# Masks and biases written into PSUM banks by ScalarE, and TensorE's turn rotated, in an attention and feed-forward kernel

## The chip, the cores and the metric

The kernel runs on one core of a Trainium2 chip. The metric is the device time of one execution in microseconds. Engines are named as in the profile: PE (TensorE), DVE (VectorE), ACT (ScalarE), POOL (GpSimd), SP (the queue that issues DMAs). "Bank" is one of PE's eight result banks in PSUM, 128 partitions by 512 words of fp32.

## The reference, cut to what matters

Tokens come from an image tensor (512 x 8 rows) and a text tensor (77 x 8 rows): 4712 tokens with 256 features. Three steps follow, each with fp32 weights.

```python
h = einsum('bhid,oi,od->bho', x, weighted_sum, weight)       # image tokens
h = concatenate([h, txt], axis=1)
# attention over the 8 batch entries of one token position, 16 heads of 16
qkv = layernorm(h) @ in_w.T + in_b;  q, k, v = split(qkv)
att = softmax(einsum(norm(q), norm(k)) * exp(min(logit_scale, log 100)))
h = h + ((att @ v) * head_scale) @ out_w.T + out_b
# feed-forward: attention among the 16 heads of one token, then 8 gated experts
y = layernorm(h);  g = rmsnorm(y) * gamma1
q = g @ Wq + bq;  k, v = split((g @ Wdown + bdown) @ Wup + bup)
x2 = y + (softmax(q k^T / 4) v) @ Wo + bo
h2 = rmsnorm(x2) * gamma2;  gate = softmax(h2 @ Wg + bg)
out = h + x2 + sum_e gate_e * (h2 @ We_e)
```

In both steps a token attends to a few others only: in the first to the 8 rows of its own position, in the second a head to the heads of its own token. The kernel computes scores for blocks of 32 rows and adds a mask of -2^120 to the scores that don't belong.

## The kernel before, in words

The 4712 tokens are cut into 37 tiles of 128 rows. The program has three parts: the first makes the image tokens and splits the weights into a high and a low fp16 part; the second runs the attention step over all tiles; the third runs the feed-forward step. A product in fp32 accuracy is three fp16 products (`product`, lines 173 to 179), two chunks of 128 features each, so six matmuls.

The second and third part are software pipelines with the order written by hand. Each engine has its own function `body(i, p)`, run once a turn by `tiles_in_order` (line 59): a few turns unrolled ahead, a hardware loop over the middle, the rest unrolled behind. In turn `i` an engine works on several tiles at different depths; `real(i, k)` is true where tile `i + k` exists. Every engine carries out its own list strictly in order, and waits on counters (semaphores) with `wait_ge`; there is no planner. In the last turns of the attention part each engine appends the first turns of the feed-forward part (`in_tail`, turns 35 and later).

Attention, turn `i`, on PE (lines 885 to 923): for tile i a mask product into bank b_s (L889, 4 rows by 512 columns in bf16, with `start=True`), on top of it the scores (L881, 64 small 32x32-tile matmuls); the output product of tile i-2 (rows_times, L176 to L178); transposes of xn of tile i+3 (L904); the weighted sums of tile i-1 (L871, 128 small ones); the product that makes q and k of tile i+2 into b_qk, ended by the bias product (L185, ones by the bias row, 3 rows by 512 columns); the V product of tile i+2 into b_v; the transposes of on of tile i-1 (L920). ACT (lines 935 to 964) makes xn, the exp (L946), the square and the copy of q and k out of b_qk (L950, L952), the high half of xn transposed (xt_h, L956), the high half of on transposed (on_t_h, L960) and the V copy (vaug, L964). DVE (lines 978 to 1056) makes the maximum (smax, L981), the subtraction (sc, L992), the transposes, the normalisation and the low halves (on_t_l L1053, xt_l L1056); POOL does three Newton steps for the norms (L1076).

Feed-forward, turn `i`, on PE (lines 604 to 669): the mask product of tile i into bank b_s3 (L607) and the first half of the scores (L589); the transposes of on of tile i-1 (L616); the q product of tile i+1; the second half of the scores; then the four expert products of tile i-2 with the other small products between them, the transposes of h (L655) and of hn (L661), and last the gate product of tile i-1 (with its bias, L185). ACT: on_t_h (L678), qraw (L682), the exp (L686), lat (L690) and lat_h (L694) of tile i+1, and more. DVE: on_t_l (L750), smax (L754), sc (L757), the expert sums (acc and res, L742), lat_l (L763), pr_t, x, fq_t, kv_t, v, h (L789), of (L793), h_t_l (L798), on (L803), hn_l, hn, the gate's maximum and normalisation.

Of the kernel before, what the change touches and what calls it, by code (L numbers as in the profile page):

```python
# [86 lines left out]
def build(nc, x, txt, wst_in, w_rep, in_w, logit, head, out_w, g1, wq, wd, bd, wu, bu, bv, bo, bq,  # L87
          wo, g2, wg, we, biases, bscale_c, ident_c, amask_c, fmask_c, out):
    with ExitStack() as ctx, ExitStack() as phase1:
# [44 lines left out]
        v48 = [sb(f"v48_{p}", [P, 16, 48]) for p in range(2)]  # L134

# [37 lines left out]
        def product(dst, a_h, a_l, b_h, b_l, chunks, start=True, stop=True):  # L173

            for c in range(chunks):
                nc.tensor.matmul(dst, a_h(c), b_h(c), start=start and c == 0, stop=False)  # L176
                nc.tensor.matmul(dst, a_h(c), b_l(c), start=False, stop=False)  # L177
                last = nc.tensor.matmul(dst, a_l(c), b_h(c), start=False, stop=stop and c == chunks - 1)  # L178
            return last

        def rows_times(dst, t_h, t_l, w_h, w_l, bias=None):

            last = product(dst, lambda c: t_h[:, c, :], lambda c: t_l[:, c, :], w_h, w_l, KC, stop=bias is None)
            if bias is not None:
                last = nc.tensor.matmul(dst, ones3[:, :], brow[:, bias], start=False, stop=True)  # L185
            return last
# [49 lines left out]
        with nc.Block() as block:  # L236
# [215 lines left out]
            def _(pe):  # L452
# [13 lines left out]
                for i in range(IMG_TILES):  # L466
# [57 lines left out]
                 "bvec_ps", "bvec_ready")  # L524
# [3 lines left out]
         bvec_ps, bvec_ready) = map(sem, names)  # L528
# [5 lines left out]
        def ffn_coefficients(pool, j):  # L534
# [31 lines left out]
                 "f_gmul", "f_we", "f_comb", "f_acc", "f_x1", "p_x1", "p_hx2", "p_t2", "p_r2", "out_done")  # L566
# [3 lines left out]
         f_gmul, f_we, f_comb, f_acc, f_x1, p_x1, p_hx2, p_t2, p_r2, out_done) = map(sem, names)  # L570
# [5 lines left out]
        def ffn_pe(pe):  # L576
# [27 lines left out]
            def body(i, p):  # L604
                if real(i, 0):
                    pe.wait_ge(f_qt, i + 1)
                    nc.tensor.matmul(b_s3[:, :], fm[:, 0:P], fm[:, P:], start=True, stop=True,  # L607
                                     skip_group_check=True)
                    scores(range(0, 8))
                if real(i, -1):  # L610
                    pe.wait_ge(f_on, i)
                    wait(pe, f_h2l, i - 1)
                    if real(i, 0):
                        pe.wait_ge(f_lat, i + 1)
                    for c in range(KC):
# [57 lines left out]
        def ffn_act(act):  # L673
            def body(i, p):
# [182 lines left out]
        with nc.Block() as block:  # L857
            @block.tensor
            def _(pe):
# [25 lines left out]
                def body(i, p):  # L885
                    if real(i, 0):
                        pe.wait_ge(a_qkt, i + 1)
                        wait(pe, a_sub, i)
                        nc.tensor.matmul(b_s[:, :], am[:, 0:P], am[:, P:], start=True, stop=True,  # L889
                                         skip_group_check=True)  # L890
                        scores(range(0, 4))
# [16 lines left out]
                    if real(i, 2):  # L908
                        pe.wait_ge(a_xtl, i + 3)
                        wait(pe, a_qkr, i + 2)  # L910
                        rows_times(b_qk[:, :], xt_h, xt_l, lambda c: inw_h[:, c, 0:2 * D],
                                   lambda c: inw_l[:, c, 0:2 * D], slice(0, 2 * D)).then_inc(a_qkm, 1)
                    if real(i, 2):
                        wait(pe, a_v, i + 2)
                        rows_times(b_v[:, 0:D], xt_h, xt_l, lambda c: inw_h[:, c, 2 * D:3 * D],
                                   lambda c: inw_l[:, c, 2 * D:3 * D]).then_inc(a_vm, 1)
                    if real(i, -1):
                        pe.wait_ge(a_on, i)
                        for c in range(KC):
# [7 lines left out]
                           slice(3 * D, 4 * D)).then_inc(bvec_ps, 1)  # L927
                head = ffn_pe(pe)
# [3 lines left out]
            def _(act):  # L932
                nc.scalar.activation(ls[:, :], ls[:, :], ACT.Exp).then_inc(ls_ready, 1)

                def body(i, p):
                    if real(i, 3):
# [5 lines left out]
                                             scale=cf_all[:, at, RS:RS + 1].squeeze(1)).then_inc(a_xn, 1)  # L942
                    if real(i, 0):
                        act.wait_ge(a_sub, i + 1)
                        wait(act, a_prt, i)
                        nc.scalar.activation(pr[:, :, :], sc[:, :, :], ACT.Exp).then_inc(a_exp, 1)  # L946
                    if real(i, 2):
# [4 lines left out]
                        nc.scalar.activation(qkr[(p + 2) % 3][:, :], b_qk[:, :], ACT.Copy, scale=1.0 / WS).then_inc(a_qkr, 1)  # L952
                    if real(i, 3):
# [235 lines left out]
```

## Time and profile before

| | us |
|---|---|
| median of 3 runs | 916.53 |
| lowest, highest | 912.55, 917.62 |
| the profiled execution | 916.73 |
| its span | 914.9 |

Over that span PE is busy 808.9 us (88%), DVE 787.8 (86%), POOL 398.9 (44%), ACT 321.7 (35%). The first part lasts until about 100 us, attention until about 390, feed-forward from about 410 to the end, with a mixed stretch between them. A matmul's end is modelled, so two neighbours on PE may overlap in the rows. "PEclk" is TensorE's granted clock, 1.00 for 2.4 GHz.

### The profile page before, as it was taken

Reading aid. Unit: us, or ns where it says so; the run is one execution under the profiler, and the core shown is the slowest. Engines: PE = TensorE matmul, PEld = TensorE weight load, DVE = VectorE, ACT = ScalarE, POOL = GpSimd, SP = SyncE. Lnnn points to the kernel's source line nnn. Section 1 sums busy time; section 2 is a strip of 40 time slices with the busy share of each in tenths; the row PEclk is TensorE's granted clock in tenths of the full one; section 3 lists DMA queues with packets and bytes.
Section 4 is the critical chain, followed back from the end, with each engine's and each line's share of the span. In section 5 each row is a group of like instructions: output and inputs, shape, how many; then the busy total and the mean of one; then the engine's idle time right before and its main releaser. Section 6 shows DMA issues by size and latency. Waiting matters only on the chain.

```text
span 914.9 us, 48709 instructions
## 1 busy us (share of the span) xinstructions
PE 808.9 (88%) x20422; PEld 517.0 (57%) x20422; DVE 787.8 (86%) x1847; ACT 321.7 (35%) x797; POOL 398.9 (44%) x1122
## 2 busy tenths in 40 slices
PE   4999788888888888776999999999999999999997
PEld 3888455555555555444555555555555555555553
DVE  5898479999999999856789999999999999999996
ACT  4576334444444444212222322332233223322321
POOL 1421255555555555644334444434443344434111
PEclk9999989999999999857899999999999999999999
DMA  9973000000000000000000000000000000000000
GB/s 324 312 239 110 2 3 4 0 0 0 0 0 0 0 0 1 4 2 4 9 10 13 12 11 6 11 11 11 6 11 11 11 6 11 11 6 11 12 16 17
DMA packets 16692, 28.14 MB, mean 31 GB/s; under 512 B 3425, under 2 KB 11953, under 8 KB 16632
## 3 DMA queue, kind: packets, MB, share of 16 engines
q1 hardware_dynamic: 16632, 27.28, 9.0%
q8 instruction: 45, 0.74, 0.3%
q14 instruction: 15, 0.12, 0.0%
HBM read 22.44 MB, written 4.83 MB: 30 GB/s over the span
## 4 chain that ended last, share of the span: by engine, by line
DVE 27%; PE 15%; issue 10%; ACT 3%; DVEq 1%; POOL 1%; ACTq 0%; POOLq 0%
PE bank L589 6%; DVE acc L742 5%; DVE fq_t L778 3%; DVE h L789 3%; DVE smax L754 3%; DVE sc L757 3%; DVE pr_t L767 2%; DVE of L793 2%; PE bank L176 2%; DVE kv_t L780 2%; PE bank L177 2%; PE bank L178 1%; DVE x L774 1%; PE bank L616 1%; DVE h_t_l L798 1%
## 5 line engine op out<-in xcount | busy, mean ns | idle before, releaser
L833 POOL TENSOR_TENSOR qpad<-qraw,bq_s 128x256 f32<-128x256 f32 x37 | 26.8, 725 | 200.7 <-ACT qraw L682 200.7
L176 PE MATMUL bank<-we_h,h_t_h 128*128 128x512 f16 x296 | 113.8, 384 | 0.0
L177 PE MATMUL bank<-we_l,h_t_h 128*128 128x512 f16 x296 | 112.7, 381 | 0.0
L178 PE MATMUL bank<-we_h,h_t_l 128*128 128x512 f16 x296 | 112.5, 380 | 0.0
L742 DVE SCALAR_TENSOR_TENSOR acc<-bank,gate,acc 128x256 f32<-128x256 f32 x222 | 105.1, 474 | 5.1 <-PE bank L178 1.1
L176 PE MATMUL bank<-tokw_h,x_t_h 128*128 128x256 f16 x256 | 70.7, 276 | 12.2 <-DVE x_t_l L371 12.2
L177 PE MATMUL bank<-tokw_l,x_t_h 128*128 128x256 f16 x256 | 70.6, 276 | 0.0
L178 PE MATMUL bank<-tokw_h,x_t_l 128*128 128x256 f16 x256 | 70.5, 276 | 0.0
L600 PEld LDWEIGHTS bank<-pr_t,v 32*32 32x32 f32 x4736 | 48.0, 106 | 33.0 <-issue 33.0
L1076 POOL TENSOR_TENSOR rt<-rn 128x32 f32<-128x32 f32 x111 | 26.7, 240 | 84.7 <-DVE rn L1048 78.9
L946 ACT ACTIVATE pr<-sc 128x512 f32<-128x512 f32 x37 | 23.3, 630 | 108.0 <-DVE sc L992 108.0
L589 PEld LDWEIGHTS bank<-kv_t,fq_t 32*32 32x32 f32 x4736 | 49.3, 108 | 18.4 <-issue 18.4
L589 PE MATMUL bank<-kv_t,fq_t 32*32 32x32 f32 x4736 | 57.9, 196 | 0.6 <-issue 0.6
L600 PE MATMUL bank<-pr_t,v 32*32 32x32 f32 x4736 | 56.2, 195 | 2.4 <-issue 2.4
L871 PE MATMUL bank<-vaug,pr_t 32*32 32x17 f32 x4736 | 49.3, 183 | 4.2 <-issue 4.2
L871 PEld LDWEIGHTS bank<-vaug,pr_t 32*32 32x32 f32 x4736 | 45.2, 108 | 9.8 <-issue 9.8
L176 PE MATMUL bank<-inw_h,xt_h 128*128 128x512 f16 (+1 forms) x148 | 50.5, 341 | 0.0
L178 PE MATMUL bank<-inw_h,xt_l 128*128 128x512 f16 (+1 forms) x148 | 49.9, 337 | 0.0
L177 PE MATMUL bank<-inw_l,xt_h 128*128 128x512 f16 (+1 forms) x148 | 49.8, 336 | 0.0
L178 PEld LDWEIGHTS bank<-we_h,h_t_l 128*128 128x128 f16 x296 | 29.1, 98 | 35.3 <-issue 0.6
L712 ACT ACTIVATE h_t_h<-bank 128x256 f16<-128x256 f32 x37 | 14.2, 384 | 95.9 <-PE bank L655 95.9
L371 DVE TENSOR_TENSOR x_t_l<-xbuf,x_t_h 128x1024 f16<-128x1024 f32 x32 | 39.5, 1239 | 8.4 <-ACT x_t_h L294 8.4
(204 smaller groups left out, 2275.5 us busy)
## 6 DMA issues: line engine op xcount, KB each, us to landing
xbuf<-in_x SPq DMA_DIRECT2D x32, 512.0 KB, 4.6
out<-res SPq DMA_DIRECT2D x36, 128.0 KB
we_s<-in_we SPq DMA_DIRECT2D x4, 512.0 KB, 5.6
inw<-in_in_w SPq DMA_DIRECT2D x1, 768.0 KB, 11.4
wrep<-in_w_rep SPq DMA_DIRECT2D x1, 512.0 KB, 5.4
h_all<-in_txt SPq DMA_DIRECT2D x1, 512.0 KB
wst<-in_wst_in SPq DMA_DIRECT2D x1, 256.0 KB, 2.8
outw<-in_out_w SPq DMA_DIRECT2D x1, 256.0 KB, 10.6
```

Of the source, the lines that this page charges most:

```text
L176: nc.tensor.matmul(dst, a_h(c), b_h(c), start=start and c == 0, stop=False)
L177: nc.tensor.matmul(dst, a_h(c), b_l(c), start=False, stop=False)
L178: last = nc.tensor.matmul(dst, a_l(c), b_h(c), start=False, stop=stop and c == chunks - 1)
L371: nc.vector.tensor_tensor(x_t[i % XT][1][:, :, :], xbuf[i % XB][:, :, :], x_t[i % XT][0][:, :, :], ALU.subtract).then_inc(lo_ready, 1)
L589: last = nc.tensor.matmul(b_s3[q, pair * 32:pair * 32 + 32], fq_t[q, 2 * pair:2 * pair + 2, :].rearrange("r t h -> r (t h)"), kv_t[q, :, 2 ...
L600: last = nc.tensor.matmul(b_o3[q, pair * 32:pair * 32 + 32], v48[p][q, pair, 16:48], pr_t[0][q, pair, :], start=True, stop=True)
L742: op = nc.vector.scalar_tensor_tensor(out=(res if e == E - 1 else acc)[:, :], in0=b_we[s % 2][:, k * D:(k + 1) * D], scalar=gate[p][:, e:e ...
L754: nc.vector.tensor_reduce(smax[:, :], s3, AX.X, ALU.max).then_inc(f_max, 1)
L757: nc.vector.tensor_tensor(sc[:, :, :], s3, smax[:, :].unsqueeze(2).to_broadcast([P, 16, 32]), ALU.subtract).then_inc(f_sub, 1)
L778: nc.vector.transpose(fq_t[:, :, :].rearrange("r t h -> r h t"), qpad[:, :, :])
L789: nc.vector.tensor_scalar(h2[:, :], x2[:, :], r2[:, :], None, ALU.mult).then_inc(f_h2, 1)
L871: last = nc.tensor.matmul(b_o[q, h * 17:h * 17 + 17], pr_t[(p + 2) % 3][q, h, :], vaug[(p + 2) % 3][q, h, :], start=True, stop=True)
```

## The change

Three tiles are added in SBUF: `amask`, `fmask`, `qkbias` (128 x 512 fp32). Ahead of the attention loops PE makes each mask and the bias of q and k once, as a product into a bank, and ACT copies them out to SBUF. In the loops ACT copies them from SBUF into the bank before PE's next product into it, and PE's products add onto that (`onto=True`: no `start`). In attention the mask copy follows the exp, and the bias copy follows the copy of q and k; the mask copy of the feed-forward part follows its exp and is ahead of lat. The mask product of the feed-forward part stays for tile 0. PE's order is rotated: in attention the V product (and ACT's copy of it) moves from the end of a turn to the start of the next, behind the transposes of on; in the feed-forward part the transposes of on come ahead of the first half of the scores. DVE, POOL and SP keep their lists.

```diff
+        amask = sb("amask", [P, 512])
+        fmask = sb("fmask", [P, 512])
+        qkbias = sb("qkbias", [P, 512])
...
-        def rows_times(dst, t_h, t_l, w_h, w_l, bias=None):
+        def rows_times(dst, t_h, t_l, w_h, w_l, bias=None, onto=False):
-            last = product(dst, lambda c: t_h[:, c, :], lambda c: t_l[:, c, :], w_h, w_l, KC, stop=bias is None)
+            last = product(dst, lambda c: t_h[:, c, :], lambda c: t_l[:, c, :], w_h, w_l, KC, start=not onto,
+                           stop=bias is None, onto=onto)
...
@@ ffn_pe body
-                if real(i, 0):
-                    pe.wait_ge(f_qt, i + 1)
-                    nc.tensor.matmul(b_s3[:, :], fm[:, 0:P], fm[:, P:], start=True, stop=True,
-                                     skip_group_check=True)
-                    scores(range(0, 8))
                 if real(i, -1):
                     pe.wait_ge(f_on, i)
...
                     last.then_inc(f_onps, 1)
+                if real(i, 0):
+                    settle(pe, c_in)
+                    pe.wait_ge(f_qt, i + 1)
+                    if isinstance(i, int) and i == 0:
+                        nc.tensor.matmul(b_s3[:, :], fm[:, 0:P], fm[:, P:], start=True, stop=True,
+                                         skip_group_check=True)
+                    else:
+                        pe.wait_ge(f_mask, i)
+                    scores(range(0, 8))
@@ ffn_act body, between the exp (L686) and lat (L690)
+                if real(i, 0) and real(i, 1):
+                    act.wait_ge(f_sub, i + 1)
+                    nc.scalar.activation(b_s3[:, :], fmask[:, :], ACT.Copy).then_inc(f_mask, 1)
@@ attention, PE body
+                    if real(i, 1):
+                        wait(pe, a_v, i + 1)
+                        rows_times(b_v[:, 0:D], xt_h, xt_l, lambda c: inw_h[:, c, 2 * D:3 * D],
+                                   lambda c: inw_l[:, c, 2 * D:3 * D]).then_inc(a_vm, 1)
                     if real(i, 0):
+                        settle(pe, c_in)
                         pe.wait_ge(a_qkt, i + 1)
-                        wait(pe, a_sub, i)
-                        nc.tensor.matmul(b_s[:, :], am[:, 0:P], am[:, P:], start=True, stop=True,
-                                         skip_group_check=True)
+                        pe.wait_ge(a_mask, i + 1)
                         scores(range(0, 4))
...
-                        wait(pe, a_qkr, i + 2)
+                        pe.wait_ge(a_bias, i + 3)
                         rows_times(b_qk[:, :], xt_h, xt_l, lambda c: inw_h[:, c, 0:2 * D],
-                                   lambda c: inw_l[:, c, 0:2 * D], slice(0, 2 * D)).then_inc(a_qkm, 1)
-                    if real(i, 2):
-                        wait(pe, a_v, i + 2)
-                        rows_times(b_v[:, 0:D], ...).then_inc(a_vm, 1)
+                                   lambda c: inw_l[:, c, 0:2 * D], onto=True).then_inc(a_qkm, 1)
@@ attention, PE and ACT ahead of the loops
+                nc.tensor.matmul(b_s[:, :], am[:, 0:P], am[:, P:], start=True, stop=True)
+                nc.tensor.matmul(b_ot[:, :], fm[:, 0:P], fm[:, P:], start=True, stop=True)
+                nc.tensor.matmul(b_qk[:, :], ones3[:, :], brow[:, 0:2 * D], start=True, stop=True).then_inc(mask_ps, 1)
...
+                act.wait_ge(mask_ps, 1)
+                nc.scalar.activation(qkbias[:, :], b_qk[:, :], ACT.Copy)
+                nc.scalar.activation(amask[:, :], b_s[:, :], ACT.Copy)
+                nc.scalar.activation(fmask[:, :], b_ot[:, :], ACT.Copy).then_inc(mask_ready, 1)
+                act.wait_ge(mask_ready, 1)
@@ attention, ACT body
+                    if real(i, 1):
+                        act.wait_ge(a_vm, i + 2)
+                        wait(act, a_av, i - 1)
+                        nc.scalar.activation(vaug[(p + 1) % 3][:, :, 0:HD], b_v[:, 0:D], ACT.Copy, scale=1.0 / WS).then_inc(a_v, 1)
                     if real(i, 0):
...
                         nc.scalar.activation(pr[:, :, :], sc[:, :, :], ACT.Exp).then_inc(a_exp, 1)
+                    if real(i, 1):
+                        wait(act, a_sub, i + 1)
+                        nc.scalar.activation(b_s[:, :], amask[:, :], ACT.Copy).then_inc(a_mask, 1)
...
+                    if real(i, 3):
+                        wait(act, a_qkr, i + 3)
+                        nc.scalar.activation(b_qk[:, :], qkbias[:, :], ACT.Copy).then_inc(a_bias, 1)
...
-                    if real(i, 2):
-                        act.wait_ge(a_vm, i + 3)
-                        wait(act, a_av, i)
-                        nc.scalar.activation(vaug[(p + 2) % 3][:, :, 0:HD], b_v[:, 0:D], ACT.Copy, scale=1.0 / WS).then_inc(a_v, 1)
```

## Rows read from the trace of the kernel before

**Rows 1.** The page: busy us (share of the span) xinstructions; the granted clock in 40 slices.

```profile
PE 808.9 (88%) x20422; PEld 517.0 (57%) x20422; DVE 787.8 (86%) x1847; ACT 321.7 (35%) x797; POOL 398.9 (44%) x1122
...
PEclk9999989999999999857899999999999999999999
```

**Rows 2.** The chain of waits, two feed-forward turns: start us, us, what.

```profile
506.98 0.70 DVE smax L754
...
508.97 0.35 ACT lat L690
...
509.35 0.32 ACT lat_h L694
...
509.69 0.04 DVE lat_l L763
...
516.53 0.37 DVE h_t_l L798
...
517.44 0.38 PE bank L607
...
533.39 0.70 DVE smax L754
```

**Rows 3.** Waits of DVE in 470 to 880: waited for, us in total, times, longest us.

```profile
DVE smax L754 <- PE bank L589: 11.2, 31, 0.5
DVE lat_l L763 <- ACT lat_h L694: 5.2, 17, 0.3
DVE on_t_l L750 <- ACT on_t_h L678: 3.6, 15, 0.3
```

**Rows 4.** The timeline of a feed-forward turn: start us, us, engine line op.

```profile
508.43 0.63 ACT L686 ACTIVATE pr<-sc 128x512 f32<-128x512 f32 x1 [1.76 <-DVE sc L757]
...
517.75 0.75 PE L589 MATMUL bank<-kv_t,fq_t 32*32 32x32 f32 x64
...
519.53 0.42 DVE L750 TENSOR_TENSOR on_t_l<-bank,on_t_h 128x256 f16<-128x256 f32 x1 [0.24 <-ACT on_t_h L678]
...
520.27 0.69 DVE L754 TENSOR_REDUCE smax<-bank 128x16 f32<-128x512 f32 x1 [0.31 <-PE bank L589]
```

**Rows 5.** The timeline of an attention turn.

```profile
250.42 1.10 PE L881 MATMUL bank<-k_t,q_t 32*32 32x64 f32 x64
...
251.91 0.69 DVE L981 TENSOR_REDUCE smax<-bank 128x16 f32<-128x512 f32 x1
...
255.62 0.28 PE L176 MATMUL bank<-inw_h,xt_h 128*128 128x256 f16 x1
...
256.17 0.27 PE L178 MATMUL bank<-inw_h,xt_l 128*128 128x256 f16 x1
256.27 0.41 DVE L1028 TENSOR_TENSOR on<-bank,rsum 128x256 f32<-128x256 f32 x1
...
256.73 0.44 PE L920 MATMUL bank<-ident,on 128*128 128x128 f32 x2 [0.29 <-DVE on L1028]
...
258.75 0.42 DVE L1053 TENSOR_TENSOR on_t_l<-bank,on_t_h 128x256 f16<-128x256 f32 x1
...
259.42 0.68 DVE L981 TENSOR_REDUCE smax<-bank 128x16 f32<-128x512 f32 x1
```

**Rows 6.** Groups by line and shape: busy us, mean ns, idle before.

```profile
L952 ACT ACTIVATE qkr<-bank 128x512 f32<-128x512 f32 x37 | 21.9, 592 | 0.0
```

**Rows 7.** The timeline ahead of the loops.

```profile
100.09 0.59 ACT L940 ACTIVATE xn<-h_all,cf_all 128x256 f32<-128x256 f32 x1
...
100.95 0.44 PE L904 MATMUL bank<-ident,xn 128*128 128x128 f32 x2
```

**Rows 8.** Busy us (xinstructions) of each engine, then clock and DMA, in three stretches.

```profile
372.60:376.60 4.00, 2.37 (x136) 1.87 (x137) 3.58 (x11) 0.63 (x1) 2.91 (x13) 1.00 0.01 4
376.60:379.60 3.00, 3.00 (x9) 0.92 (x8) 2.09 (x5) 0.28 (x1) 1.40 (x2) 0.53 0.02 5
256.20:260.20 4.00, 3.07 (x78) 1.98 (x75) 3.80 (x11) 2.11 (x6) 1.73 (x5) 1.00 0.00 0
```

More of the change, by code:

```diff
@@ L171, in build, with product @@
         bank = [ctx.enter_context(nc.psum_tensor(f"bank{n}", [P, 512], F32)) for n in range(8)]
-        def product(dst, a_h, a_l, b_h, b_l, chunks, start=True, stop=True):
+        def product(dst, a_h, a_l, b_h, b_l, chunks, start=True, stop=True, onto=False):
             for c in range(chunks):
-                nc.tensor.matmul(dst, a_h(c), b_h(c), start=start and c == 0, stop=False)
-                nc.tensor.matmul(dst, a_h(c), b_l(c), start=False, stop=False)
-                last = nc.tensor.matmul(dst, a_l(c), b_h(c), start=False, stop=stop and c == chunks - 1)
-            return last
-        def rows_times(dst, t_h, t_l, w_h, w_l, bias=None):
-            last = product(dst, lambda c: t_h[:, c, :], lambda c: t_l[:, c, :], w_h, w_l, KC, stop=bias is None)
+                nc.tensor.matmul(dst, a_h(c), b_h(c), start=start and c == 0, stop=False, skip_group_check=onto)
+                nc.tensor.matmul(dst, a_h(c), b_l(c), start=False, stop=False, skip_group_check=onto)
+                last = nc.tensor.matmul(dst, a_l(c), b_h(c), start=False, stop=stop and c == chunks - 1,
+                                        skip_group_check=onto)
+            return last
+        def rows_times(dst, t_h, t_l, w_h, w_l, bias=None, onto=False):
+            last = product(dst, lambda c: t_h[:, c, :], lambda c: t_l[:, c, :], w_h, w_l, KC, start=not onto,
+                           stop=bias is None, onto=onto)
             if bias is not None:
@@ L523, in build @@
                  "a_on", "a_onps", "a_onh", "a_onl", "a_out", "a_h", "a_st", "a_mv", "a_keep", "p_newton", "p_rn", "p_kpad", "p_bias",
-                 "bvec_ps", "bvec_ready")
+                 "bvec_ps", "bvec_ready", "mask_ps", "mask_ready", "a_mask", "a_bias")
         (ls_ready, a_xn, a_xnps, a_xth, a_xtl, a_qkm, a_vm, a_sq, a_qkr, a_v, a_ss, a_half,
@@ L527, in build @@
          a_on, a_onps, a_onh, a_onl, a_out, a_h, a_st, a_mv, a_keep, p_newton, p_rn, p_kpad, p_bias,
-         bvec_ps, bvec_ready) = map(sem, names)
+         bvec_ps, bvec_ready, mask_ps, mask_ready, a_mask, a_bias) = map(sem, names)
         b_xt, b_qk, b_v, b_s, b_o, b_ot, b_out = bank[0:7]
@@ L565, in build @@
                  "f_wo", "f_x2", "f_ss2", "f_h2", "f_h2ps", "f_h2h", "f_h2l", "f_gate", "f_gmax", "f_gexp", "f_grec",
-                 "f_gmul", "f_we", "f_comb", "f_acc", "f_x1", "p_x1", "p_hx2", "p_t2", "p_r2", "out_done")
+                 "f_gmul", "f_we", "f_comb", "f_acc", "f_x1", "p_x1", "p_hx2", "p_t2", "p_r2", "f_mask", "out_done")
         (f_hn, f_hnps, f_hth, f_htl, f_q, f_down, f_lat, f_lath, f_latl, f_qraw, f_qpad, f_kv, f_kvt, f_qt,
@@ L569, in build @@
          f_wo, f_x2, f_ss2, f_h2, f_h2ps, f_h2h, f_h2l, f_gate, f_gmax, f_gexp, f_grec,
-         f_gmul, f_we, f_comb, f_acc, f_x1, p_x1, p_hx2, p_t2, p_r2, out_done) = map(sem, names)
+         f_gmul, f_we, f_comb, f_acc, f_x1, p_x1, p_hx2, p_t2, p_r2, f_mask, out_done) = map(sem, names)
         b_turn, b_q, b_kv, b_we, b_s3, b_o3, b_hn = bank[0], bank[1], bank[2], bank[3:5], bank[5], bank[6], bank[7]
@@ L909, in body @@
                         pe.wait_ge(a_xtl, i + 3)
-                        wait(pe, a_qkr, i + 2)
+                        pe.wait_ge(a_bias, i + 3)
                         rows_times(b_qk[:, :], xt_h, xt_l, lambda c: inw_h[:, c, 0:2 * D],
-                                   lambda c: inw_l[:, c, 0:2 * D], slice(0, 2 * D)).then_inc(a_qkm, 1)
-                    if real(i, 2):
-                        wait(pe, a_v, i + 2)
-                        rows_times(b_v[:, 0:D], xt_h, xt_l, lambda c: inw_h[:, c, 2 * D:3 * D],
-                                   lambda c: inw_l[:, c, 2 * D:3 * D]).then_inc(a_vm, 1)
+                                   lambda c: inw_l[:, c, 0:2 * D], onto=True).then_inc(a_qkm, 1)
                     if real(i, -1):
```

## The prediction

> **What bounds the kernel now.** I began with the page: how busy each engine is, and the clock that TensorE was granted. PE is busy 88% of the span, DVE 86%, ACT 35% [rows 1]. So PE and DVE both look nearly full, and ScalarE looks free. That is an average over two long stages, and a thing moved to a free engine costs nothing only where nobody waits for that engine. So I read one turn of each stage.
>
> *Second stage (feed-forward), from about 410 us to the end.* The chain of waits repeats every turn. Two turns go from a smax start at 506.98 to one at 533.39, 13.2 us each [rows 2]. In each turn the chain runs smax, sc on DVE, then **ACT's exp, lat and lat_h**, and back to DVE at lat_l. From there it stays on DVE to h_t_l, crosses to PE for the gate product, the mask product (L607), the first half of the scores, the transposes, the q product and the second half of the scores, and ends at the next smax. The reader is to see two things. The mask product is on the chain. And so is ScalarE, exactly once, between exp and lat_h: lat starts 0.54 us after exp starts and lat_l starts as lat_h ends [rows 2, 4]. DVE's waits say the same: in the steady stretch DVE waited 11.2 us in 31 turns for PE's scores, 5.2 us in 17 turns for lat_h, and 3.6 us in 15 turns for on_t_h [rows 3]. In the turns without a shown wait at lat_l, lat_h ends just as DVE gets there.
>
> *First stage (attention), about 112 to 390 us.* One turn takes 7.51 us (smax at 251.91 and at 259.42) [rows 5]. The scores end at 251.52 (250.42 plus 1.10) and smax starts 0.39 later, because DVE is still at earlier work. PE in its turn is idle 0.29 us ahead of the transposes of on, waiting for DVE. DVE sets the pace here, with almost no wait of its own.
>
> **The change part by part.** No DMA is added, removed or moved.
>
> (a) *Feed-forward mask copy, placed between exp and lat on ScalarE.* It runs in 36 turns (tiles 0 to 35; the next tile's mask). Its wait (f_sub) is already met when exp starts, so it follows exp at once. Behind it in ScalarE's queue are lat and lat_h, and for those waits DVE at lat_l; behind lat_l stand pr_t, two acc, x, fq_t, kv_t, v, h, two acc, of, h_t_l, all on the chain. So what the copy takes is added to the turn in full. The trace has no ScalarE write into a bank. The nearest row by shape and source is exp, 512 elements from SBUF: 0.63 us long, with the next operation 0.54 us after its start [rows 2, 4], an overlap of 0.09. The ends: a 512-element copy of 0.592 us out of a bank [rows 6], less the same overlap, is 0.50; exp's full 0.63 if nothing overlaps. A gain is excluded, since ScalarE does one thing at a time. I take 0.54, as exp shares the source: 36 x 0.54 = **+19.4 us** (18.0 to 22.7).
>
> The Trainium skill (ScalarE: Activation LUTs, "Step-by-step: what each stage is for") says that a ScalarE result goes faster into PSUM than into SBUF, and under "What ACT_TABLE_LOAD costs" it gives 186 ns + 0.833 ns per element, less about 93 ns between neighbours: an estimate of 0.52 us from that page, or 18.7 us in 36 turns. No row here shows a write to a bank.
>
> (b) *Feed-forward mask product gone from 36 turns, the transposes of on put ahead of the scores.* L607 starts at 517.44, the scores at 517.75: 0.31 [rows 2, 4]. Nothing else of PE's segment goes; two transposes and eight groups of scores change places. The transposes can start when on is ready, which it is by the end of the gate product, so the swap itself costs about nothing. It helps once: the transposes no longer stand behind 0.7 us of scores, so on_t_h is there before DVE wants it and the 0.24 us wait at on_t_l goes. What is late next is still PE: with the scores 0.31 earlier, smax can start at 519.96 instead of 520.27, while DVE, ready for on_t_l at 519.29, would have been done at 519.71 [rows 4]. So of the two improvements only PE's counts, and I take 0.30 per turn. The ends: 0.21, if going from transposes to the small score tiles costs PE some 0.1 more than from L607 to them; 0.38, all of L607. 36 x 0.30 = 10.8; two of these turns run while the clock is low [rows 1], where L607 costs about twice, 0.5 more: **-11.3 us** (7.6 to 13.7).
>
> (c) *Attention: mask product and bias product gone from PE, two copies added on ScalarE.* PE's work falls by about 0.3 + 0.3 us a turn. Since the scores already end 0.39 ahead of smax [rows 5], DVE gains nothing. The mask copy stands behind exp and ahead of the square of q and k, which waits for PE's product anyway; the bias copy fills a stretch in which ScalarE would wait for V. Cost 0.
>
> (d) *Attention rotation: the V product moves behind the transposes of on.* After the q/k product PE has nothing until DVE's on ends at 256.68 (256.27 plus 0.41); the transposes start at 256.73; V takes 0.82 (255.62 to 256.17 plus 0.27) [rows 5] and would run 257.02 to 257.85. Queued behind V is xt_h on ScalarE, behind xt_h is on_t_h, and for that waits DVE at on_t_l, 258.75 [rows 5]. xt_h would start about 257.9, on_t_h 0.28 later, ending 258.55: 0.2 us before DVE wants it. The cover is thin but there. If it were gone, each 0.1 us missing costs 3.4 us in 34 turns. I take 0, with ends of -1 (less traffic) and +4.
>
> (e) *Before the loops.* ScalarE's first xn starts at 100.09 now [rows 7]. After the change it stands behind three copies, which wait for three more products on PE. PE is free for these at 100.95, where the first transposes start now [rows 7]. Three products of 512 columns with about 0.25 between starts and 0.38 for the last end near 101.85. Three copies at 0.54, 0.54 and 0.6 end near 103.5, and xn follows: **+3.4 us** (3.1 to 3.8). Every engine stands idle for it, nothing hides it.
>
> (f) *Filling and draining the pipeline.* There PE's products are on the path: two bias products, and three or four mask products, at 0.3 each at full clock and up to 0.5 at half. About half of them should count: **-1.5 us** (-2.5 to 0).
>
> Sum: 19.4 - 11.3 + 0 + 3.4 - 1.5 = +10.0 us. The profiled execution took 916.73 (its span is 914.9, and 1.8 lies around it); the median of the runs shown is 916.53, 0.2 less. Forecast: 926.7 on the first footing, **926.5 us** as a median.
>
> **The rivals.**
>
> *1. PE is the bound of the feed-forward stage, and the result is faster.* The mechanism: the 0.5 us that lat_l comes later is absorbed in DVE's queue before h_t_l, so only (b) counts. For it: PE is busy 88% against DVE's 86% [rows 1], and it is the scores that DVE waits for most [rows 3]. Against it: the chain has no wait between lat_l (509.69) and h_t_l (516.53) in which DVE is free [rows 2]. It would decide if DVE had over 0.24 us of slack there. Time: 916.5 - 11.3 + 3.4 - 1.5 = 907.
>
> *2. The two sides of the feed-forward turn cancel.* Copy at 0.50, PE's segment shorter by 0.38, and the fill and drain gain their full 2.5: 18.0 - 13.7 + 3.1 - 2.5 = +4.9, or 921; another microsecond from the attention stage gives 920, inside 0.5%.
>
> *3. The attention stage slows down by its rotation.* on_t_h comes 0.2 us after DVE wants it rather than before. Then each of 34 turns costs 0.2: 926.5 + 7 = 933. For it: two more copies in ScalarE's queue, and a thin cover. Against it: the arithmetic of (d).
>
> *4. TensorE's clock falls in the attention stage.* Ahead of a fall from 2.4 to 1.2 GHz near the end of this stage PE was busy 2.37 of 4.00 us; an idle-rich stretch of a steady turn has 3.07 of 4.00, at a granted clock of 1.00 [rows 8]. The change takes the mask product out of just that stretch and puts an idle 1.3 us (255.4 to 256.7) ahead of the transposes, some 0.3 us less work than now. That goes towards the stretch that fell without reaching it. At half clock PE's turn would take about 10 us instead of 7.5; ten such turns cost 25 us: 951. The Trainium skill (TensorE: Matmul & The Clock Gate, its Part 1, the HAM clock gate) says that the throttled state is the default and that activity releases it; the fall behind the emptier stretch agrees.
>
> That the copies would not do what they say (a bank's sum not starting from what ScalarE wrote) would change the numbers, not the time.
>
> **How the numbers follow.** The forecast gets 0.69, rival 1 0.09, rival 2 0.08, rival 3 0.09, rival 4 0.05. What a measurement of this kernel can tell from no change is about 0.5%, 4.6 us. The forecast's own ends are +3.9 (18.0 - 13.7 + 3.1 - 2.5 - 1) and +22.9 (22.7 - 7.6 + 3.8 + 4), 920.4 to 939.4, which are all bad luck on one side; its middle takes in 921 to 934. The range is 919 to 936: it holds the forecast but for its far end, rival 2 and rival 3, and leaves out rivals 1 and 4. Slower by over 0.5%: nearly all of the forecast, rivals 3 and 4, a little of rival 2: 0.81. Within 0.5%: most of rival 2, the low end of the forecast, a part of rival 1: 0.11. Faster: 0.08.
>
> **What would show each step.** (a): the copy in the feed-forward turn lasting 0.55 to 0.63 us; lat starting 1.0 to 1.1 us after exp instead of 0.54; DVE waiting for lat_h in every turn, 0.5 to 0.8 us each, the largest of its waits. (b): DVE's waits for on_t_h gone, those for the scores still there; PE's segment from h_t_l to smax 0.3 shorter. Both: a feed-forward turn of about 13.45 us. (c), (d): an attention turn of 7.5 to 7.6 us, no new wait of DVE in it, on_t_l without idle before it. (e): the first xn near 103.5. The prediction is wrong if the feed-forward turn is not longer than 13.2 us, if DVE's wait at lat_l has not grown, if the attention turn changes by more than 0.1 us, or if the granted clock leaves 1.0 in a stage where it was steady.

## The result, and the profile after

The changed kernel takes 939.0 us (median of 4, 937.4 to 939.8); the kernel before 915.4 beside it (median of 4). The ratio is 1.0263, 95% interval 1.0236 to 1.0289: slower by about 24 us. Medians and ratios, here and below, leave out the few executions in which the chip was in a slower state. The direction was forecast, the size was not: 926.5 us, range 919 to 936. The profiled execution took 938.91 us with a span of 937.1, 22.2 more than before.

The page, busy times and granted clock:

```profile
PE 781.1 (83%) x20315; PEld 512.9 (55%) x20315; DVE 787.2 (84%) x1847; ACT 380.1 (41%) x910; POOL 396.4 (42%) x1122
...
PEclk9999889999999999755999999999999999999999
```

Against [rows 1], PE lost 28 us of work and ScalarE took on 58, as the change says, and the span grew by 22.

The chain of waits over two feed-forward turns (start us, us, what):

```profile
527.68 0.70 DVE smax L766
...
529.67 0.58 ACT bank L698
530.25 0.29 ACT lat L702
...
530.57 0.32 ACT lat_h L706
...
530.91 0.04 DVE lat_l L775
...
537.83 0.37 DVE h_t_l L810
...
538.65 0.37 PE bank L616 x2
539.02 0.68 PE bank L594 x55
539.71 0.08 issue
539.78 0.27 PE bank L179
...
540.60 0.70 PE bank L594 x56
...
541.33 0.70 DVE smax L766
...
555.08 0.70 DVE smax L766
```

A turn is 13.65 and 13.75 us here against 13.2 in [rows 2]. The new entry is `ACT bank L698`, the mask copy, between exp and lat. From a smax to its lat_l it is 3.23 us (527.68 to 530.91); in [rows 2] it was 2.71 (506.98 to 509.69). That is 0.52 more, in every turn. The other half of the turn is the surprise: from h_t_l's start to the next smax it was 3.74 (516.53 to 520.27, [rows 2, 4]) and 3.50 in the other kind of turn, and is 3.50 (537.83 to 541.33) and 3.73 now. The mask product is gone from that stretch and nothing became shorter.

The waits of DVE in 480 to 900 us (us in total, times, longest), to be held against [rows 3]:

```profile
DVE lat_l L775 <- ACT lat_h L706: 21.1, 30, 0.8
DVE smax L766 <- PE bank L594: 12.2, 31, 1.6
DVE acc L754 <- PE bank L181: 3.5, 14, 0.3
DVE on_t_l L762 <- issue: 3.4, 14, 0.3
```

The wait at lat_l has gone from 5.2 us in 17 turns to 21.1 in 30: it is now the largest. The wait for PE's scores is as large as before. The 0.24 us ahead of on_t_l is still there, and its releaser is now "issue": what DVE waits for there, in one turn of two, is nothing on another engine. Run 12 below ties it to the jump of DVE's own loop.

The timeline of an attention turn, as in [rows 5]:

```profile
301.70 0.69 DVE L1006 TENSOR_REDUCE smax<-bank 128x16 f32<-128x512 f32 x1
...
305.98 0.41 DVE L1053 TENSOR_TENSOR on<-bank,rsum 128x256 f32<-128x256 f32 x1
...
306.45 0.44 PE L931 MATMUL bank<-ident,on 128*128 128x128 f32 x2 [1.29 <-DVE on L1053]
...
307.27 0.27 PE L181 MATMUL bank<-inw_h,xt_l 128*128 128x256 f16 x1
...
307.92 0.38 ACT L989 ACTIVATE on_t_h<-bank 128x256 f16<-128x256 f32 x1
...
308.46 0.42 DVE L1078 TENSOR_TENSOR on_t_l<-bank,on_t_h 128x256 f16<-128x256 f32 x1
...
309.13 0.68 DVE L1006 TENSOR_REDUCE smax<-bank 128x16 f32<-128x512 f32 x1
```

The turn is 7.43 between these two smax, and 7.564 on average over turns 14 to 32, against 7.567 before. PE's idle time ahead of the transposes of on is 1.29 us, V ends at 307.54, on_t_h ends at 308.30 and DVE takes it at 308.46: the thin cover held, with 0.16 us to spare.

Ahead of the loops, and the first stretch of the attention part (timeline; then busy times, granted clock 0.76, DMA):

```profile
101.36 0.60 ACT L949 ACTIVATE qkbias<-bank 128x512 f32<-128x512 f32 x1 [1.53 <-PE bank L941]
...
102.33 0.60 ACT L951 ACTIVATE fmask<-bank 128x512 f32<-128x512 f32 x1
102.97 0.60 ACT L959 ACTIVATE xn<-h_all,cf_all 128x256 f32<-128x256 f32 x1
...
103.62 0.68 PE L919 MATMUL bank<-ident,xn 128*128 128x128 f32 x2 [2.30 <-ACT xn L959]
...
105.78 0.63 PE L179 MATMUL bank<-inw_h,xt_h 128*128 128x512 f16 x1
```

```profile
100.00:120.00 20.00, 12.00 (x108) 6.37 (x106) 7.30 (x18) 9.69 (x21) 7.07 (x23) 0.76 0.00 1
```

The first xn starts at 102.97, 2.88 later than in [rows 7]. But the first smax of the attention part is at 118.38 against 114.12, 4.26 later. The further 1.4 us come with the clock, as far as the rows show; no run separates the two. PE stood idle 2.3 us for the copies, and its first q/k and V products run at half clock: the granted clock is 0.50 from 104 to 110, a matmul takes 0.63 us that took 0.38 before, and from the first of these products to the end of the last it is 4.1 us instead of 2.5. The kernel before has a low stretch as well, but it is shorter and in the second tile's products (granted clock 0.78, 0.50 and 0.87 in the three 2 us windows from 106); the changed kernel has a second one from 116 to 120 (0.83, 0.50).

### The profile page after: what moved, and what is told of

It is laid out like the page before. It is cut to its first block, busy times and chain, and to the rows that moved or that the text cites. A ratio compares the mean times of both kernels' runs of the same rounds, so it can differ in the third digit from the quotient of the medians.

```text
span 937.1 us, 48668 instructions
## 1 busy us (share of the span) xinstructions
PE 781.1 (83%) x20315; PEld 512.9 (55%) x20315; DVE 787.2 (84%) x1847; ACT 380.1 (41%) x910; POOL 396.4 (42%) x1122
## 4 chain that ended last, share of the span: by engine, by line
DVE 27%; PE 13%; issue 10%; ACT 5%; DVEq 1%; POOL 1%; ACTq 0%; POOLq 0%
PE bank L594 6%; DVE acc L754 5%; DVE fq_t L790 3%; DVE h L801 3%; DVE smax L766 3%; DVE sc L769 3%; DVE pr_t L779 3%; PE bank L179 2%; DVE of L805 2%; ACT bank L698 2%; DVE kv_t L792 2%; PE bank L616 2%; DVE x L786 1%; DVE h_t_l L810 1%; PE bank L181 1%
## 5 line engine op out<-in xcount | busy, mean ns | idle before, releaser
L931 PE MATMUL bank<-ident,on 128*128 128x128 f32 x74 | 17.3, 318 | 47.5 <-DVE on L1053 47.5
L969 ACT ACTIVATE pr<-sc 128x512 f32<-128x512 f32 x37 | 23.3, 630 | 77.4 <-DVE sc L1017 77.4
L695 ACT ACTIVATE pr<-sc 128x512 f32<-128x512 f32 x37 | 23.3, 630 | 68.1 <-DVE sc L769 68.1
```

## The experiments

"Turn" is the mean feed-forward turn: the start of smax in turn 33 less that in turn 5, divided by 28. "Inner" and "edge" are the two kinds of turn: PE's hardware loop is two turns long, and an edge turn is one whose first operation comes behind the loop's jump. The columns after them give where, in us from the first gate product of the turn, PE starts the first scores and the q product, and DVE the next smax (from one turn of each kind in the timeline; inner / edge).

Five of the means hold turns that are 0.59 us shorter for a reason of their own, which the last section shows: one such turn in the changed kernel, in run 1 and in run 8, two in run 6, three in run 12. Without them the means are 13.70 (changed), 13.18 (run 1), 13.07 (run 8), 13.20 (run 6) and 13.16 (run 12).

| kernel | turn | scores | q product | smax |
|---|---|---|---|---|
| before | 13.199 | 0.58 / 0.80 | 1.54 / 1.76 | 3.08 / 3.30 |
| changed | 13.680 | 0.71 / 1.03 | 1.54 / 1.73 | 3.08 / 3.27 |
| 1 copy behind lat_h | 13.156 | 0.71 / 1.03 | 1.54 / 1.73 | 3.08 / 3.28 |
| 2 and order back | 13.211 | 0.37 / 0.80 | 1.54 / 1.78 | 3.08 / 3.32 |
| 4 small mask product | 13.091 | 0.37 / 0.58 | 1.54 / 1.57 | 3.08 / 3.11 |
| 5 and gmax early | 13.037 | 0.37 / 0.59 | 1.33 / 1.54 | 2.88 / 3.21 |
| 6 gmax early | 13.156 | 0.58 / 0.80 | 1.54 / 1.76 | 3.08 / 3.30 |
| 7 loop edge moved | 13.131 | 0.58 / 0.58 | 1.54 / 1.54 | 3.08 / 3.08 |
| 8 three together | 13.047 | 0.34 / 0.34 | 1.30 / 1.30 | 2.87 / 3.20 |
| 9 rotation alone | 13.454 | 1.03 / 1.34 | 1.71 / 2.05 | 3.27 / 3.60 |

**1. The copy behind lat_h.**

```diff
@@ changed kernel, ffn_act body
-                if real(i, 0) and real(i, 1):
-                    act.wait_ge(f_sub, i + 1)
-                    nc.scalar.activation(b_s3[:, :], fmask[:, :], ACT.Copy).then_inc(f_mask, 1)
                 if real(i, 1):
                     ...
                     nc.scalar.activation(lat_h[:, :], lat[:, :], ACT.Copy).then_inc(f_lath, 1)
+                if real(i, 0) and real(i, 1):
+                    ... (the same three lines)
```

> The changed kernel with one edit: in the feed-forward part ScalarE's mask copy stands behind lat_h instead of between exp and lat. Theory 1 (place of the copy): the copy's 0.52 us of pitch was added to the turn in full because lat and lat_h stand behind it and DVE waits for them; behind lat_h nobody waits for it. The feed-forward turn falls from 13.68 to 13.16-13.20 us, DVE's wait at lat_l returns to about 0.3 in every second turn, and the time to 919-922 us (939 less 36 x 0.52). Rival 2 (load of ScalarE and of the banks: more writes slow the others wherever the copy stands): the turn stays at 13.6 or above, 935-939 us.

Measured: 920.5 us against 914.5, ratio 1.0070 (1.0047 to 1.0093); the turn is back at 13.16. DVE's waits in 490 to 880 us:

```profile
DVE smax L766 <- PE bank L594: 12.2, 30, 2.1
DVE lat_l L775 <- ACT lat_h L703: 4.6, 15, 0.3
```

The same operations, one moved by two places in a queue, are worth 18 us. The load of the banks (rival 2) is out.

**2. PE's order taken back as well.**

```diff
@@ ffn_pe body, on top of run 1: this block now ahead of the transposes of on
+                    else:
+                        pe.wait_ge(f_mask, i)
+                        nc.tensor.matmul(b_s3[:, 0:8], fm[:, 0:P], fm[:, P:P + 8], start=False, stop=True, ...)
+                    scores(range(0, 8))
```

> As the run before, and PE's order in the feed-forward part taken back: first half of the scores ahead of the transposes of on; the scores' wait is carried by a product of 8 columns that adds the mask once more to the first 8 columns (in every turn but the first), in place of the 512-column product. Theory A (two gates): the 0.3 us that the absent mask product should give is held back in every second turn by the q product's wait for gexp (gate and q share a bank), so the gain over the run before is about 0.25 us in one kind of turn and 0.03 in the other, 0.14 on average: 915 us, turn 13.05. Rival B (the swap alone ate it, by changes between large and small tiles): taking it back frees 0.25-0.30 in every turn: 910 us, turn 12.9. Rival C (PE is not what smax waits for any more): no change, 920.

Measured: 920.5 against 914.5, ratio 1.0072 (1.0050 to 1.0094), no gain over run 1. Theory A's 915 us and its turn of 13.05 did not come (13.21); the number is rival C's, for another reason than rival C's. In the inner turn the scores start 0.34 earlier and the q product not at all, which is the hold that theory A speaks of. In the edge turn the small product starts at 0.60 where the large one started at 0.48 in the kernel before, so that the scores are no earlier; that its second wait (for the mask) does this I only suppose.

**3. The attention part alone** (feed-forward as before).

> The change in the attention part alone (with all three copies ahead of the loops); the feed-forward part as before. Prediction's terms (c), (d), (e): attention turn unchanged at 7.57 us and 3.4-4.3 us lost ahead of the loops: 919-921 us. If the rotation or the added copies cost something in the mixed stretch or in filling, more than that: 923 or above.

Measured: 919.0 against 914.5, ratio 1.0049 (1.0033 to 1.0066). The attention turn is 7.545 and the feed-forward turn 13.19, so neither stage lost anything. The first smax of the attention part is 3.8 us late, which is most of the loss; one long turn at the end of the feed-forward loop (14.34 us) adds about 1.1, and the filling between the parts gives some back. Run 1's total is 1.5 us above this one, though its feed-forward turn is no longer; the two intervals overlap, and no run says more.

**4. The mask product cut to 8 columns in the kernel before.**

```diff
-                    nc.tensor.matmul(b_s3[:, :], fm[:, 0:P], fm[:, P:], start=True, stop=True,
+                    nc.tensor.matmul(b_s3[:, 0:8], fm[:, 0:P], fm[:, P:P + 8], start=True, stop=True,
```

> The kernel before, with the feed-forward mask product cut from 512 to 8 columns (the mask is left out beyond these): the price of that product on the path, with nothing added. Theory A (gexp holds the q product in every second turn): 0.22 us less in one kind of turn, 0.03-0.05 in the other: 5 us in 37 turns, 911 us. Rival B (the product is on the path in full): 0.22-0.30 in every turn, 8-11 us, 905-908 us.

Measured: 911.0 against 914.5, ratio 0.9965 (0.9952 to 0.9979), theory A's number. An inner turn's timeline:

```profile
578.80 0.18 PE L176 MATMUL bank<-wg_h,h_t_h 128*128 128x8 f16 x1 [0.15 <-DVE h_t_l L798]
...
579.08 0.16 PE L607 MATMUL bank<-fm 2*128 2x8 bf16 x1
...
579.17 0.75 PE L589 MATMUL bank<-kv_t,fq_t 32*32 32x32 f32 x64
...
579.85 0.44 PE L616 MATMUL bank<-ident,on 128*128 128x128 f32 x2
580.00 0.19 ACT L720 ACTIVATION_READ_ACCUMULATOR gexp<-bank,gmax 128x1 f32 x1
...
580.34 0.27 PE L176 MATMUL bank<-wq_h,hn_t_h 128*128 128x256 f16 x1
```

The scores start at 0.37 instead of 0.58, the transposes at 579.85. In the kernel before the q product follows the transposes after 0.28; here it follows after 0.49, at 580.34, which is 0.15 us after ScalarE has read the gate's sum (580.00 plus 0.19). `b_gate` lies in the bank of q (`b_q[:, D:D + E]`), and the q product waits for `f_gexp`. In the inner turns of the kernel before, both came at the same time and hid each other.

**5 and 6. gmax ahead of hn on DVE**, with the small mask product (5) and alone (6).

```diff
@@ ffn_dve body
+                if real(i, -1):
+                    dve.wait_ge(f_gate, i)
+                    nc.vector.tensor_reduce(gmax[:, :], b_gate, AX.X, ALU.max, negate=True).then_inc(f_gmax, 1)
                 if real(i, 3):
                     ... (hn, L813)
-                (the gmax lines)
```

> The kernel before with the feed-forward mask product cut to 8 columns (mask left out beyond these) and one more edit: DVE takes the gate's maximum (gmax) ahead of hn instead of behind it, so that gexp ends about 0.33 us earlier. Theory A (in every second turn the q product waits for gexp, 1.54 us after the gate product, whatever PE saved): released, the q product starts at about 1.30 in that kind of turn, smax 0.24 earlier there and not at all in the other kind: turn 12.97 us against 13.09 with the small mask product alone, time 906-908 us. Rival (something else holds the q product at 1.54): no change, 911.

> The kernel before with only gmax ahead of hn on DVE. Theory A: nothing changes, since with the full mask product PE itself reaches the q product at 1.51 and 1.75 us: turn 13.20, 914-916 us. If gexp were the gate in the kernel before as well, every second turn would be 0.2 shorter: 911.

Measured: 5 takes 910.3 against 917.0, ratio 0.9918 (0.9899 to 0.9937); 6 takes 915.2, ratio 0.9985 (0.9973 to 0.9997). An inner turn of 5:

```profile
579.68 0.18 PE L176 MATMUL bank<-wg_h,h_t_h 128*128 128x8 f16 x1 [0.15 <-DVE h_t_l L798]
...
580.05 0.75 PE L589 MATMUL bank<-kv_t,fq_t 32*32 32x32 f32 x64
...
580.56 0.19 ACT L720 ACTIVATION_READ_ACCUMULATOR gexp<-bank,gmax 128x1 f32 x1
...
580.73 0.44 PE L616 MATMUL bank<-ident,on 128*128 128x128 f32 x2
...
581.01 0.27 PE L176 MATMUL bank<-wq_h,hn_t_h 128*128 128x256 f16 x1
```

gexp is read 0.32 us earlier and the q product starts at 1.33: released, and only here, since 6 leaves all of these starts where they were. Theory A's hold is shown; its numbers are not reached (turn 13.04 against 12.97, 910.3 us against 906 to 908). In run 6 the two shorter turns account for the lower mean: without them it is 13.20, as before. The edge turn shows the next limit: the second scores start at 2.29, 0.03 earlier than in run 4, where smax followed at 3.11; here it starts at 3.21, without a wait for PE: DVE is not there sooner. The edit itself does that, as run 8 shows.

**7. The loop's edge on PE moved.**

```diff
@@ ffn_pe: back() is the part of body() from the transposes of h on
+            def turn(i, p):
+                if not (isinstance(i, int) and i == 0):
+                    back(i - 1, 1 - p)
+                body(i, p)
...
-                tiles_in_order(pe, ffn_pe(pe), 2, 3, start=0)
+                tiles_in_order(pe, turn, 2, 3, start=0)
+                back(TILES + 1, (TILES + 1) % 2)
```

> The kernel before with PE's feed-forward turns cut elsewhere: the same instructions in the same order, but the edge of the hardware loop (two turns long) lies ahead of the transposes of h, where PE waits for DVE anyway, instead of between the gate product and the mask product. Theory E: the mask product starts 0.48 us after the gate product in one kind of turn and 0.27 in the other because the loop's edge is there; moved, both are 0.27, one turn in two is 0.22 shorter: turn 13.09-13.10 us, 911-912 us. Rival (the two kinds of turn differ by a buffer or by DVE's side): no change, 915.

Measured: 914.1 against 917.0, ratio 0.9969 (0.9951 to 0.9986). The turn is 13.13, and what was the edge turn now reads:

```profile
592.53 0.18 PE L176 MATMUL bank<-wg_h,h_t_h 128*128 128x8 f16 x1 [0.23 <-DVE h_t_l L808]
...
592.81 0.37 PE L607 MATMUL bank<-fm 2*128 2x512 bf16 x1
...
593.11 0.49 PE L589 MATMUL bank<-kv_t,fq_t 32*32 32x32 f32 x34
```

The mask product starts 0.28 after the gate product (0.48 before), as in the other turn. Same instructions, same order, 0.2 us in every second turn: the jump of the loop. The turn is a little longer than the 13.09 to 13.10 expected, and the time 2 us longer than the 911 to 912.

**8 and 12. Versions put together.** 8 has the mask copy behind lat_h, PE's old order without the mask product, gmax early and the moved edge, attention as before. 12 has gmax early, the moved edge and DVE's loop four turns long (`tiles_in_order(dve, lambda i, p: turn(i, p % 2), 2, 3, unroll=4, start=0)`), the mask product as before.

> The kernel before with: the feed-forward mask copied by ScalarE behind lat_h (from an SBUF copy made once in the attention part's second turn), no mask product but for tile 0, PE's order as before (scores ahead of the transposes), gmax ahead of hn, and the loop edge of PE moved. Attention as before. Theories 1, A and E together: the scores start 0.28-0.30 us after the gate product in both kinds of turn, the q product at 1.25, smax 0.25-0.5 earlier: turn 12.85 us, 902-904 us, faster than both kernels. If one of the three theories fails: 907-912.

> The kernel before with three reorderings and no change of work: gmax ahead of hn on DVE, PE's loop edge ahead of the transposes of h, and DVE's feed-forward loop four turns long instead of two (half as many edges on DVE, whose first operation after an edge stood idle 0.24-0.3 us). Edges theory: 13.13 us from the PE edge, less about 0.06-0.12 from half of DVE's edges: turn 13.03, 910-912 us, faster than both kernels. If DVE's idle at its edge is no edge cost: 913-914.

Measured: 8 takes 915.0 against 917.0, ratio 0.9989 (0.9970 to 1.0009); 12 takes 911.4 against 913.6, ratio 0.9991 (0.9971 to 1.0012). Neither shows a gain, and run 8 is far above the 902 to 904 us expected. Run 12's 911.4 lies in the range that I gave, but the kernel before beside it took 913.6, and the turn without the three shorter ones is 13.16, not 13.03. Of DVE's waits ahead of on_t_l in 480 to 880 us, 7 are left of run 7's 15: with half as many jumps in DVE's loop there are half as many, so the 0.24 us belongs to that jump.

In 8 all starts on PE are where they should be (0.34, 1.30 in both kinds), but smax is at 3.20 in every second turn, without a wait for PE. DVE is the bound then, and what made it so is the early gmax. Behind gmax, hn does not start at once:

```profile
620.60 0.41 DVE L834 TENSOR_SCALAR hn<-h_all,cf_all 128x256 f32 x1 [0.26 <-issue]
```

Here hn starts 0.87 us after the gate product and the next acc at 1.20; in run 7, with hn ahead of gmax, they start at 0.44 and 0.84. on_t_l in the edge turn is at 2.87 instead of 2.51. So runs 5, 8 and 12, which all start acc at 1.20, pay about 0.3 us on DVE for the earlier gexp. What the mask copy could give with the gate's sum early and DVE not delayed, for instance with the gate product in a bank of its own, no run shows. With all three edits the turn is 13.07 against 13.20, and 0.07 of that is run 7's edit alone. Of the kernels that leave nothing out, run 7 has the lowest ratio, 0.3% under the kernel before. Its interval excludes 1, but run 12, which contains its edit, does not repeat the gain in its total time.

**9. The rotation alone.**

```diff
@@ kernel before, ffn_pe body: the block of the transposes of on moved ahead of
                 if real(i, 0):
                     pe.wait_ge(f_qt, i + 1)
                     nc.tensor.matmul(b_s3[:, :], fm[:, 0:P], fm[:, P:], start=True, ...)
```

> The kernel before with PE's feed-forward order rotated and nothing else: transposes of on, then the mask product, then the first half of the scores. It asks what the rotation costs while the mask product is still there. By the rows of the changed kernel (transposes at 0.35 and 0.66 us after the gate product, 0.36 to the next group) the mask product starts at 0.6-0.7 and 0.95, the scores at 1.0 and 1.3, the q product at 1.7 and 2.0: smax 0.15 and 0.3 later, turn 13.42 us, 923-925 us. If the rotation costs nothing (the prediction's step b), 13.2 us and 915-917.

Measured: 924.8 against 913.6, ratio 1.0105 (1.0070 to 1.0140); turn 13.45. An inner turn:

```profile
585.42 0.18 PE L176 MATMUL bank<-wg_h,h_t_h 128*128 128x8 f16 x1 [0.15 <-DVE h_t_l L798]
...
585.76 0.44 PE L611 MATMUL bank<-ident,on 128*128 128x128 f32 x2
...
586.13 0.38 PE L617 MATMUL bank<-fm 2*128 2x512 bf16 x1
...
586.45 0.75 PE L589 MATMUL bank<-kv_t,fq_t 32*32 32x32 f32 x64
...
587.13 0.28 PE L176 MATMUL bank<-wq_h,hn_t_h 128*128 128x256 f16 x1
```

This is the run that finds the failed step. The rotation costs 0.255 us a turn (13.454 less 13.199): smax comes 0.19 us later in an inner turn and 0.30 in an edge turn. Taking the mask product away from the rotated order (run 9 to run 1) gives 0.28 (13.45 less 13.18): 0.19 and 0.32 by the smax column. The gain was there nearly as forecast; the rotation ate it. The inner turn's gain would be larger without gexp: from the first scores to the q product it is 0.68 in run 9 and 0.83 in run 1 and in the changed kernel, so there too the q product is held at 1.54. (Run 1 also has the copy behind lat_h in these turns, which nobody waits for.)

**10. Half of the copy** (changed kernel, `b_s3[:, 0:256]` from `fmask[:, 0:256]`).

> The changed kernel with ScalarE's feed-forward mask copy cut to 256 of 512 columns (the other half of the mask is left as it was), in its place between exp and lat. If the copy's length is on the path one for one, each turn is 0.21 us shorter (exp's and the copies' rows give 0.83 ns per column): turn 13.47 us, 930-932 us. If its place costs a fixed hand-over rather than its length, 936-939.

Measured: 930.6 against 913.6, ratio 1.0165 (1.0125 to 1.0205); turn 13.497. The copies of the changed kernel and of this one (ns min/median/max):

```profile
L698 ACT ACTIVATE bank<-fmask x36: 582/583/584, 419.8 to 899.6; 128x512 f32<-128x512 f32 x36
```

```profile
L698 ACT ACTIVATE bank<-fmask x36: 369/370/371, 420.3 to 893.7; 128x256 f32<-128x256 f32 x36
```

0.213 us shorter copies, 0.20 us shorter turns (13.70 less 13.50, without the shorter turn of the changed kernel): its length is on the path one for one.

**11. What lies ahead of the loops, alone** (three products, three copies, used by nobody; PE waits for them too).

> The kernel before with the three products and three copies ahead of the loops, used by nobody, and PE as well as ScalarE waiting for them; loops as before. The prediction's term (e): the first xn about 3.1-3.4 us later and all else shifted by as much: 918-920 us. If the fill of the pipeline takes it up: under 917.

Measured: 918.4 against 913.6, ratio 1.0043 (1.0025 to 1.0062): some 4 us, about what run 3 lost. Here too the first products run at half clock (0.50 from 104 to 108); the first smax is 5.8 us late, and part of that is made up later.

## Why the prediction was wrong, step by step

- *(a), right.* 0.54 us a turn was taken, 0.52 came. The copy lasted 0.583, longer than its share of the turn by the overlap that was assumed. Its place on the chain was read from [rows 2] correctly, runs 1 and 10 show it.
- *(b), wrong, and this is the miss.* The step said that "the swap itself costs about nothing" and counted -0.30 a turn, -11.3 us. The mask product's part was nearly right: 0.28. The swap costs 0.255. Net of both, 13.18 (run 1) against 13.20, under 1 us in 36 turns, not 11.3. The rows of runs 7 and 9 show of what it is made. In an inner turn the transposes start 0.34 after the gate product where the mask product started at 0.27, and from them to the next group is 0.37 where it was 0.28 with the q product behind them. In an edge turn the transposes start at 0.66, the mask product at 0.48: 0.32 late against 0.21, so the jump weighs more with the transposes and their three waits at its head. I had looked at one edge turn only (517.44). Its 0.31 between mask product and scores is the same in both kinds, but gexp holds the q product in the inner turns alone.
- *(b), second part, wrong too.* "What is late next is still PE" left out a second gate. With or without the rotation, the q product waits for gexp in each inner turn once the mask product is gone or small (the changed kernel, runs 1, 2 and 4; released in 5). And the 0.24 us ahead of on_t_l, put down to on_t_h in [rows 3], did not go: it belongs to the jump of DVE's loop (run 12).
- *(c) and (d), right.* Attention turn 7.56 before and after, margin 0.16 us where 0.2 was worked out. Rivals 3 and 4 did not come in the steady stage.
- *(e) and (f), mis-sized.* Together +1.9 us was forecast, and +4.3 stood at the first smax, +4.1 at the last smax of the attention part and +3.6 at the first of the feed-forward part. The copies cost 2.88, less than the 3.4 of (e), but the first products then ran at half clock; the other 1.4 us at the first smax came with that. Of the -1.5 of (f) at most 0.7 showed.
- *Not foreseen.* Where the changed kernel's loop ends, one turn (smax at 869.42, the next at 884.18) is 1.0 us longer than its neighbours; in it PE stops for 1.00 us in the middle of a group of 64 like matmuls, with "issue" as the releaser. Runs 1, 5 and 10 have such a stop, and run 3 too (1.10 us), whose feed-forward part is that of the kernel before; that kernel and run 2 have none. So neither the mask copy nor the rotation there makes it. I take it for something tied to where the code lies; no run settled it.

The sum of what was measured: +18.7 for (a), -0.8 for (b), +3.6 at the first smax of the feed-forward part, +1.0 at the loop's end and -0.6 for the one shorter turn is 21.9 for a span that grew by 22.2. Of the 12 us between forecast and result, some 10 are step (b).

## What to carry to other kernels

A shared queue in order is a chain of its own: before work goes to an engine that is 35% busy, read which of its operations are on the chain, and put the new one behind the last of them, not ahead of the first. An exchange of two operations on an engine that bounds the stage is never free by default: price it with the gap ahead of each in both orders, and in each kind of turn of an unrolled loop. And before a product is counted as removed time, look for the waits that now end at the same moment as it: they will be next. Last, look at each turn before you compare means: one shorter turn of 0.59 us in 28 moves a mean by 0.02, as much as all that was left of step (b).

## What the runs showed of the hardware that was not expected

- PE's first operation behind the jump of its loop came 0.21 us late where that was the mask product (0.48 against 0.27 after the gate product) and 0.32 late where it was the transposes (0.66 against 0.34). Run 2's small product, with two waits ahead of it, came 0.32 late as well (0.60 against 0.28), so it may be the waits that weigh and not the kind of product. With the jump ahead of a wait (run 7) every turn is 13.13, the length of the inner turns before. DVE's jump cost it 0.24 us.
- Behind 2.3 us of idle PE ahead of the loops, the first products ran at half clock (0.63 us instead of 0.38), and 2.9 us of copies became 4.3 us at the first smax.
- DVE's h and POOL's x1b start within 0.07 us of each other (turns 5 to 33 of the kernel before, the changed one and runs 1, 6, 8 and 12: 168 turns). In 160 of them h lasts 0.81 to 0.90 us and x1b 0.72 to 0.74. In the eight shorter turns named above, h lasts 0.31 and x1b 0.87 or 0.88. Two turns of run 6, one behind the other, the first of them such a turn:

```profile
500.02 0.31 DVE L789 TENSOR_SCALAR h<-x,r 128x256 f32<-128x256 f32 x1
500.05 0.87 POOL L850 TENSOR_TENSOR x1b<-x,bo_s 128x256 f32<-128x256 f32 x1
...
512.51 0.72 POOL L850 TENSOR_TENSOR x1b<-x,bo_s 128x256 f32<-128x256 f32 x1
512.57 0.81 DVE L789 TENSOR_SCALAR h<-x,r 128x256 f32<-128x256 f32 x1
```

  The rows read as if one of the two holds up the other, and the turn is 0.59 us shorter when h gets ahead. That is more than the mask copy costs (0.52 a turn), and it is in both kernels in nearly every turn. No run moved x1b, so the cause is not shown.
- A ScalarE copy of 128 x 512 words from SBUF into a bank took 0.583 us; out of a bank it takes 0.592 [rows 6]. With 256 columns it took 0.370, so 0.83 ns a column and about 0.16 us fixed. The Trainium skill (ScalarE: Activation LUTs, under "What ACT_TABLE_LOAD costs") gives 0.833 ns per element and 186 ns fixed: the slope agrees, the fixed part into a bank was 0.03 us less, in the direction of its remark that writes to PSUM are the faster ones.
